# A two-layer attention and expert kernel: router weights laid over partitions by DMA, and the gate's weighting moved to another engine

## The reference

```python
logits = jnp.dot(x, Wr) + br
aff = jax.nn.sigmoid(logits)
top_v, top_i = jax.lax.top_k(aff, K)
top_w = top_v / (jnp.sum(top_v, axis=-1, keepdims=True) + 1e-09)
w_full = jnp.zeros((T, e_total)).at[jnp.arange(T)[:, None], top_i].set(top_w)
shared = jnp.dot(silu(jnp.dot(x, Wg_s) + bg_s) * (jnp.dot(x, Wu_s) + bu_s), Wd_s) + bd_s
gate = silu(jnp.einsum('th,ehi->eti', x, Wg) + bg[:, None, :])
up = jnp.einsum('th,ehi->eti', x, Wu) + bu[:, None, :]
down = jnp.einsum('eti,eih->eth', gate * up, Wd) + bd[:, None, :]
routed = jnp.einsum('te,eth->th', w_full, down)
return (shared + routed).reshape(b, s, h)
```

## Time and profile before

| What | Value |
|---|---|
| median of 3 runs | 244.21 us (244.19 to 244.49) |
| the profiled execution, its own time | 244.43 us |
| span of that execution | 242.6 us |
| PE busy | 224.3 us (92%) |
| DVE busy | 175.9 us (72%) |
| ACT busy | 128.8 us (53%) |
| POOL busy | 74.6 us (31%) |
| granted clock of TensorE, mean over the span | 0.993 |

### The profile page before, as it was taken

One profiled execution on the slowest core, in us unless ns is written; L12 is line 12 of the kernel. 1 busy time (PEld: TensorE's weight loads), 2 busy tenths in 40 slices (PEclk: granted clock), 3 DMA queues, 4 the chain that ended last, 5 costly groups with the idle time before them and its releaser, 6 DMA issues.

```text
span 242.6 us, 3703 instructions
## 1 busy us (share of the span) xinstructions
PE 224.3 (92%) x1220; PEld 157.4 (65%) x1228; DVE 175.9 (72%) x436; ACT 128.8 (53%) x262; POOL 74.6 (31%) x113
## 2 busy tenths in 40 slices
PE   8979998999997888999999998889999999999993
PEld 2446544655564344678687966667888888888871
DVE  2689766663376887796351787999888879888883
ACT  2427557678536921442544766666454555554551
POOL 6235997020430600000490303000453353353000
PEclk9999999999999999999999999979999999999999
DMA  6316739300000000000052000000112212200002
GB/s 226 123 43 195 263 87 352 118 0 0 3 0 0 1 0 4 0 0 3 1 139 80 0 3 1 0 0 0 46 43 49 81 47 48 83 0 0 3 0 86
DMA packets 6152, 12.92 MB, mean 53 GB/s; under 512 B 1139, under 2 KB 2259, under 8 KB 5878
## 3 DMA queue, kind: packets, MB, share of 16 engines
q1 hardware_dynamic: 5302, 11.91, 15.8%
q10 hardware_dynamic: 832, 0.78, 1.0%
HBM read 10.78 MB, written 0.52 MB: 47 GB/s over the span
## 4 chain that ended last, share of the span: by engine, by line
PE 74%; DVE 18%; ACT 3%; issue 3%; POOL 1%; DVEq 0%; another core or an unknown queue 0%; ACTq 0%; POOLq 0%
PE bank L1939 6%; PE bank L1943 6%; PE bank L1940 6%; PE bank L1302 5%; PE bank L1442 5%; PE bank L1428 5%; DVE att L707 4%; PE bank L1383 4%; PE bank L1973 3%; PE bank L1789 3%; PE bank L1976 3%; PE bank L1328 3%; PE bank L1974 3%; PE bank L1954 3%; PE bank L1776 3%
## 5 line engine op out<-in xcount | busy, mean ns | idle before, releaser
L1242 ACT ACTIVATE arena_d<-bank,bias 128x512 f32<-128x512 f32 x34 | 23.4, 689 | 32.3 <-PE bank L1943 32.3
L893 DVE SCALAR_TENSOR_TENSOR arena_d<-bank,bias,arena_d 128x512 f32<-128x512 f32 x34 | 25.5, 750 | 9.5 <-ACT arena_d L1242 9.2
L572 DVE TENSOR_REDUCE smax<-bank 128x3 f32<-128x462 f32 (+2 forms) x44 | 25.2, 619 | 8.4 <-PE bank L1383 8.3
L1054 ACT ACTIVATE arena_c<-bank 128x512 f32<-128x512 f32 x40 | 22.6, 598 | 10.2 <-PE bank L1442 5.4
L471 POOL CAST arena_b<-rec 128x512 fp32r<-128x512 f32 x17 | 13.4, 788 | 46.7 <-PE bank L1976 46.6
L1939 PE MATMUL bank<-arena_b 128*128 128x512 f32 x68 | 27.1, 399 | 0.1
L1943 PE MATMUL bank<-arena_b 128*128 128x512 f32 x68 | 27.1, 398 | 0.0
L1940 PE MATMUL bank<-arena_b 128*128 128x512 f32 x68 | 27.0, 397 | 0.0
L907 DVE TENSOR_TENSOR arena_a<-arena_d,arena_a 128x512 fp32r<-128x512 f32 x34 | 23.5, 691 | 0.8 <-ACT arena_a L1249 0.7
L1249 ACT CAST arena_a<-arena_d 128x512 fp32r<-128x512 f32 x34 | 20.8, 612 | 3.2 <-DVE arena_d L902 2.9
L902 DVE TENSOR_TENSOR arena_d<-arena_d,bank 128x512 f32<-128x512 f32 x32 | 21.8, 681 | 0.4 <-PE bank L1954 0.3
(11 more groups left out here) (256 smaller groups left out, 477.1 us busy)
## 6 DMA issues: line engine op xcount, KB each, us to landing
rec<-in_rec SPq DMA_DIRECT2D x17, 257.0 KB, 2.6
arena_d<-in_fc SPq DMA_DIRECT2D x1, 2048.0 KB, 9.2
fc<-in_fc SPq DMA_DIRECT2D x1, 2048.0 KB, 7.8
arena_a<-yhi SPq DMA_DIRECT2D x14, 64.0 KB, 2.0
x<-in_x SPq DMA_DIRECT2D x2, 256.0 KB, 4.2
out<-x SPq DMA_DIRECT2D x2, 256.0 KB, 2.0
arena_a<-ylo SPq DMA_DIRECT2D x7, 64.0 KB, 2.0
pack<-in_pack ACTq DMA_DIRECT2D x1, 382.0 KB, 5.6
```

Of the source, the lines that this page charges most:

```text
L572: dve.tensor_reduce(dst, src, AX.X, ALU.max).then_inc(Z["max_done"], 1)
L893: dve.scalar_tensor_tensor(to[:, k % 2, :], bank[:, 2 + k % 2, :], bias[:, u % SPLITS, 1:2], sil[:, k % 2, :], ALU.add, ALU.mult).then_inc ...
L1054: act.activation(pT[:, n % RING, :], bank[:, 3 + n % 2, :], ACT.Exp, scale=float(DH) ** -0.5)\
L1242: act.activation(sil[:, k % 2, :], bank[:, k % 2, :], f, bias=bias[:, STEPS[k][0] % SPLITS, 0:1])\
```

## The change

In the steps k = 8 to 33 ("steps 9 to 34") the matmul `router_weights` is left out. In its place:

- ACT copies the transposed router weights out of PSUM as they are (`raw_weights(b)`, in the place of `high_weights_again(b)`, whose copy goes to POOL). SP stores them into a DRAM scratch of shape (2, 32, 8, 512), eight copies of each expert's row. For each step, SP then loads a tile `laid_w` of 128x512: two experts, 64 partitions each, eight partitions from each copy. There is a ring of six such tiles and three semaphores.
- POOL multiplies `sil` by that tile, in place (`silw_ready`), and DVE's `gated(k)` takes the product in place of `sil`. `gated(k)` writes into PSUM bank 5 - k % 2, which `hidden(k)` names, and `weighted(k)` falls away. `high_hidden` and `low_hidden` read that bank.
- The splits of records 6 to 16 leave POOL: ACT casts (`high_cast`) and DVE makes the rest (`low_part`), both within the loop. `SPLITS` goes from 5 to 6, and POOL splits records 0 to 5.
- The rings of `hhi` and `hlo` go from 2 to 4, and `down` runs three steps behind `gate_and_up`, not two. `gate_and_up(k)` from k = 10 on waits for `sil_ready` for its gate and for `hh_ready` only ahead of its up part.
- The biases no longer come with the records but with the constants (`pack`, 34 more columns). Some tiles change their places, two semaphores are merged into others (`mask` into `rows`, `screst_ready` into `sclo_ready`).

```diff
@@ SP, after the constants and the first records
+            def laid_weights(k):
+                u, b = STEPS[k]
+                m = k - LAID_FROM
+                if m >= LAID_RING:
+                    sp.wait_ge(Z["hh_ready"], k - LAID_RING + 1)
+                if m >= 3:
+                    sp.wait_ge(Z["laid%d" % (m % 3)], laid_weights_count(m - 3))
+                own = wraw_d[b, 2 * (u - 1):2 * u, :, None, :].rearrange("e r j s -> (e r) j s")\
+                    .broadcast_to([2 * COPIES, I1 // COPIES, S])
+                sp.dma_start(laid_w[:, m % LAID_RING, :], own).then_inc(Z["laid%d" % (m % 3)], 16)
+            for n in range(3, SPLITS + 3):
+                record(n)
+            for b in range(B):
+                sp.wait_ge(Z["wraw_ready"], b + 1)
+                sp.dma_start(wraw_d[b], wraw[:, None, b * S:(b + 1) * S].broadcast_to([E1, COPIES, S])).then_inc(Z["stored"], 16)
+            sp.wait_ge(Z["stored"], 16 * B)
+            for k in range(LAID_FROM, NSTEP):
+                if k % 2 == 0 and SPLITS + 3 <= k // 2 + 3 < PAIRS:
+                    record(k // 2 + 3)
+                laid_weights(k)
@@ POOL, after the splits of records 0 to 5 and the four rsqrt
-            for n in range(SPLITS, PAIRS):
-                split(n)
+            for b in range(B):
+                pool.wait_ge(Z["whi_ready"], b + 1)
+                pool.tensor_copy(w3[2 * E1:3 * E1, b * S:(b + 1) * S], f32(w3[0:E1, b * S:(b + 1) * S])).then_inc(Z["w3_ready"], 1)
+            for k in range(LAID_FROM, NSTEP):
+                m = k - LAID_FROM
+                pool.wait_ge(Z["laid%d" % (m % 3)], laid_weights_count(m))
+                pool.wait_ge(Z["sil_ready"], k + 1)
+                own = laid_w[:, m % LAID_RING, :]
+                pool.tensor_tensor(own, sil[:, k % 2, :], own, ALU.mult).then_inc(Z["silw_ready"], 1)
@@ DVE, gated(k)
+                if k >= LAID_FROM:
+                    m = k - LAID_FROM
+                    dve.wait_ge(Z["silw_ready"], m + 1)
+                    dve.wait_ge(Z["hlo_ready"], k - 1)
...
+                    dve.scalar_tensor_tensor(bank[:, 5 - k % 2, :], bank[:, 2 + k % 2, :], bias[:, u, 1:2],
+                                             laid_w[:, m % LAID_RING, :], ALU.add, ALU.mult).then_inc(Z["hh_ready"], 1)
@@ DVE, new
+            def low_part(n):
+                dve.wait_ge(Z["cast_ready"], n + 1)
+                dve.tensor_tensor(wlo[:, n % SPLITS, :], rec[:, n % 3, 0:3 * P], f32(whi[:, n % SPLITS, 0:3 * P]), ALU.subtract)\
+                    .then_inc(Z["split_ready"], 1)
@@ DVE, the loop
             for k in range(8, NSTEP):
                 gated(k)
                 low_hidden(k - 1)
-                weighted(k)
+                if k % 2 == 0 and k // 2 + 2 < PAIRS:
+                    low_part(k // 2 + 2)
@@ ACT, new
+            def raw_weights(b):
+                act.wait_ge(Z["w3_ready"], 2 * (b + 1))
+                act.copy(wraw[:, b * S:(b + 1) * S], bank[0:E1, (4, 7)[b], :]).then_inc(Z["wraw_ready"], 1)
+            def high_cast(n):
+                act.wait_ge(Z["rec_ready%d" % (n % 3)], 16 * (n // 3 + 1))
+                act.wait_ge(Z["down_done"], STEPS.index((n - SPLITS, 1)) + 1)
+                act.copy(whi[:, n % SPLITS, :], rec[:, n % 3, :]).then_inc(Z["cast_ready"], 1)
@@ ACT, the loop
             for k in range(8, NSTEP):
                 silu(k)
                 high_hidden(k - 1)
+                if k % 2 == 0 and k // 2 + 2 < PAIRS:
+                    high_cast(k // 2 + 2)
@@ PE, gate_and_up(k)
                 if b == 0:
                     pe.wait_ge(Z["split_ready"], u + 1)
-                if k >= 2:
+                laid = k >= LAID_FROM + 2
+                if laid:
+                    pe.wait_ge(Z["sil_ready"], k - 1)
+                elif k >= 2:
                     pe.wait_ge(Z["hh_ready"], k - 1)
...
                 for j in range(2):
+                    if laid and j:
+                        pe.wait_ge(Z["hh_ready"], k - 1)
@@ PE, the loop
             for k in range(8, NSTEP):
                 gate_and_up(k)
-                router_weights(k)
-                down(k - 2)
+                if k > LAID_FROM:
+                    down(k - 3)
+            down(NSTEP - 3)
             down(NSTEP - 2)
```

More of the change, by code:

```diff
@@ L38 @@
 PAIRS = E1 // 2 + 1
-SPLITS = 5
+SPLITS = 6
+LAID_FROM = 8
+LAID_RING = 6
+COPIES = 8
+PARTS_RING = 4
 SIGMOIDS = 2
@@ L250, in build @@
         rec = sb("rec", [P, 3, REC])
-        bias = sb("bias", [P, SPLITS, 2])
         def f32(ap):
             return ap.bitcast(F32)
-        L = {n: sem("ld_" + n) for n in ("x0", "x1", "ctx2", "watt", "pack", "late", "rows", "gate", "fc1", "fc2", "mask", "few")}
+        L = {n: sem("ld_" + n) for n in ("x0", "x1", "ctx2", "watt", "pack", "late", "rows", "gate", "fc1", "fc2", "few")}
         names = """var_ready rstd_ready consts_ready xn_ready xnT_psum xnT_ready q_psum qhi_ready qlo_ready allhi_ready alllo_ready laid0 laid1 k_psum
@@ L311, in build, with hidden @@
         EXP_ORDER = (2, 3, 0, 1)
+        def hidden(k):
+            return bank[:, 5 - k % 2, :] if k >= LAID_FROM else hh[:, k % 2, :]
         @block.sync
@@ L320, in _ @@
             sp.dma_start(gate[:, :], gate_d).then_inc(L["gate"], 16)
-            sp.dma_start(mask[:, :, :], mask_d).then_inc(L["mask"], 16)
+            sp.dma_start(mask[:, :, :], mask_d).then_inc(L["rows"], 16)
             sp.dma_start(wout[:, :, :], wout_d).then_inc(L["few"], 16)
@@ L349, in _, with record @@
                 sp.dma_start(rec[:, n, :], rec_d[n]).then_inc(Z["rec_ready%d" % n], 16)
-            for n in range(3, PAIRS):
+            def record(n):
                 sp.wait_ge(Z["split_ready"], n - 2)
                 sp.dma_start(rec[:, n % 3, :], rec_d[n]).then_inc(Z["rec_ready%d" % (n % 3)], 16)
+            def laid_weights(k):
[18 more added lines that the diff above has]
+                laid_weights(k)
             for b in range(B):
@@ L412, in _ @@
                 expand(cc)
-            pool.wait_ge(L["mask"], 16)
+            pool.wait_ge(L["rows"], 64)
             pool.tensor_scalar(maskneg[:, :, :], mask[:, :, :], MASKED, 0.0, ALU.mult, ALU.add).then_inc(Z["maskneg_ready"], 1)
@@ L418, in _ @@
                                ALU.add).then_inc(Z["xbo_ready"], 1)
-            pool.wait_ge(L["rows"], 48)
+            pool.wait_ge(L["rows"], 64)
             pool.tensor_copy(rows3[:, :], rows[:, :]).then_inc(Z["rows_split"], 1)
@@ L1241, in silu @@
                 f = ACT.Silu if k >= SIGMOIDS else ACT.Sigmoid
-                act.activation(sil[:, k % 2, :], bank[:, k % 2, :], f, bias=bias[:, STEPS[k][0] % SPLITS, 0:1])\
+                act.activation(sil[:, k % 2, :], bank[:, k % 2, :], f, bias=bias[:, STEPS[k][0], 0:1])\
                     .then_inc(Z["sil_ready"], 1)
@@ L1246, in high_hidden @@
                 act.wait_ge(Z["hh_ready"], k + 1)
-                if k >= 2:
-                    act.wait_ge(Z["down_done"], k - 1)
-                act.copy(hhi[:, k % 2, :], hh[:, k % 2, :]).then_inc(Z["hhi_ready"], 1)
+                if k >= PARTS_RING:
+                    act.wait_ge(Z["down_done"], k - PARTS_RING + 1)
+                act.copy(hhi[:, k % PARTS_RING, :], hidden(k)).then_inc(Z["hhi_ready"], 1)
             def result(b):
@@ L1275, in _ @@
             affinities(1)
-            high_weights_again(0)
+            raw_weights(0)
             silu(2)
@@ L1282, in _ @@
             silu(4)
-            high_weights_again(1)
+            raw_weights(1)
             high_hidden(3)
@@ L2129 @@
     out = nc.dram_tensor("out_0", (P, T, D), F32, kind="ExternalOutput").ap()
-    build(nc, *args, out)
+    scratch = nc.dram_tensor("scratch", (B, E1, COPIES, S), F32).ap()
+    build(nc, *args, scratch, out)
     r = run(nc, [arrays], core_ids=[0])
```

83 lines of the change are left out of this document (44 added, 39 removed).

## The result

The kernel after the change takes 256.37 us, the median of four runs (256.29 to 257.09), against 244.35 for the kernel before on the same chip (244.19 to 244.51). The ratio is **1.0511** [1.0495, 1.0526], so 12.0 us slower, where 9.0 had been forecast; put on the 244.21 from which the forecast was counted, the ratio gives 256.7, just above the top of the range. The profiled execution took 257.09 us with a span of 255.3. PE's share of the chain, 74% before, is now 59%; DVE went from 18 to 24%, POOL from 1 to 5% and ACT from 3 to 6%.

What follows compares the result with a forecast made beforehand. PE's ten matmuls per step bound the last stage; waits for `low_part` replace them. Step 33 starts 8.45 us later, the tail makes it +8.95: 244.43 to 253.4, less 0.22 to the median, 253.2 us; range 246.8 to 256.4.

Steps and rivals of the forecast that it cites:

- What bounds the loop, and which wait replaces it: PE's ten matmuls per step bound the old loop; then PE waits at even steps 10 to 30 for DVE's `low_part`.
- As meant: Rival for the loop: weights ready whenever PE needs them, steps of 2.06 us without gaps, 238.2 us; chance 0.07.
- No block: Rival for the loop: `low_part` is not held up by POOL's product, pairs of 4.88 us, 247.2 us; chance 0.13.
- More is late: Rival: PE's clock falls in the loop (two pairs give 257.6 us) or tiles come over 1.3 us late; chance 0.12.
- A pair takes 5.48 us: Two loop steps on PE, with `low_part` held up until 0.40 after POOL's product: 5.48 us instead of 4.59.
- Its second product is early: 4.7 us: First pair, steps 8 to 10: no `down` in step 8, so POOL's second product comes early and the pair takes 4.7 us.
- ten pairs, steps 10 to 30: Loop from the start of step 10 to step 30: ten pairs of 5.48 us, 54.8 us.
- first pair: Loop from the start of step 8 to step 10: 4.7 us.
- tail, from step 33's start: End of kernel: `down(32)`'s third matmul waits for `low_hidden(32)` until 4.26 after step 33's start; +0.5 us, between 0 and 0.8.
- step 8's start, three last steps: Step 8 starts at 175.15 us; the three steps from step 30 to step 33 take 0.11 + 6.18 us.

Runs made afterwards that it cites:

- experiment 1: Changed kernel with only DVE's `low_part` moved to the head of its turn, ahead of `gated` and `low_hidden`: 238.88 us, ratio 0.979 to the kernel before.
- experiment 3: Changed kernel with `low_part` replaced by a reduction over the same 384 columns, reading one SBUF operand: 251.82 us, ratio 1.0333 to the kernel before.
- Experiment 5: Changed kernel with only `low_hidden(7)` moved ahead of `gated(8)` on DVE: 255.80 us, ratio 1.0484 to the kernel before.
- experiment 7: Changed kernel with `low_part` first, then `gated`, `low_hidden`; only `low_hidden(32)` ahead of `gated(33)`; `laid_w` 8 bytes further on: 237.56 us, ratio 0.9736 to the kernel before.
- experiment 6: Changed kernel with DVE's order `low_hidden`, `low_part`, `gated` in every turn and `laid_w` 8 bytes further on: 242.47 us, ratio 0.9941 to the kernel before.
- experiment 4: Changed kernel with the `laid_w` tiles 8 bytes further on: 254.79 us, ratio 1.0445 to the kernel before; with 64 or 32 bytes, 256.46 and 256.67 us.

## Why the prediction was right in direction and too small

**What bounds the loop, and which wait replaces it: right.** PE stands before each even step from 10 to 30 but step 12, released by `low_part`, ten waits in the list; at step 12 there are only 0.33 from matmul to matmul. `low_part` ends 0.41 after POOL's product. DVE, ACT and POOL are each below three quarters busy (at most 7.03 of 10 us from 190 to 200 us, DVE), and experiment 1 removes all of it by order alone.

**The rivals.** "As meant" fell because `low_part` stands where the forecast read it. It is what experiment 1 turns the change into: 238.88, where 238.2 had been worked out. "No block" fell by the rows of the timeline, and with experiment 3 it can be told what its world would have taken: 251.8, not 247.2. Its pairs take 5.26, not 4.88: on that path lie POOL's product (1.29 for 1.18), the handover to it (0.14 for 0.05), and the one from it to DVE (0.21 for 0.05). "More is late" was seen only at one place, a lower clock behind one wait of 2.09 us, for 0.2 us; no transfer was late.

**The sum: too small by 3.7 us** (257.09 - 244.43 = 12.66 in the profiled executions, 8.95 forecast). Two steps of the working failed. "A pair takes 5.48 us" had the path right and sizes on it too small: measured 5.73, two thirds of the 3.7. "Its second product is early: 4.7 us" left out a wait: measured 5.73, most of the rest. The terms that were mis-sized:

| term | forecast | measured | makes |
|---|---|---|---|
| ten pairs, steps 10 to 30 | 54.8 | 57.27 | +2.47 |
| first pair | 4.7 | 5.73 | +1.03 |
| tail, from step 33's start | +0.5 | +0.86 | +0.36 |
| step 8's start, three last steps (6.26 for 6.29), outside the span | | | -0.15 |

*The pairs.* Small terms, 0.25 together in the pair shown, add up ten times. POOL's product was taken as 1.18 and is 1.27 there, 1.29 in the mean: it has the length of the upper end, 0.966 scaled by columns, and not that of the straight line between two other widths. The handover from ACT to POOL was taken as 0.05 and is 0.14 (silu at 201.29 for 0.69, POOL at 202.12). The restart of PE, 2.21 instead of 2.17, is the third; three other links are 0.01 longer each.

*The first pair.* Here a wait was missing, not only a size. The 4.7 gave `low_hidden` no turn with POOL, as is right where it reads a PSUM bank; that of step 7 reads SBUF, and POOL holds it up just as it later holds up `low_part`. From the product's end to step 10 it takes 1.07 so (179.73 to 180.80), not the 0.40 + 0.05 of the forecast, which is 0.62 of what is missing; the rest is the late silu (0.27) and the longer handover and product (0.09 each); together 1.07, since the forecast's terms add up to 4.66, put as 4.7. Experiment 5 moves this instruction and wins 0.51. In experiment 3, where `low_part` has no turn to wait for, the first pair still takes 5.73 (174.53 to 180.26). Rows for it were at hand: L907 stretched by POOL to 0.82 and 0.84.

*The tail.* The wait was the right one. PE's timeline, the start of step 33 and the matmul that waits:

```profile
244.33 0.39 PE L2005 MATMUL bank<-arena_b 128*128 128x512 f32 x1
...
249.00 0.50 PE L2044 MATMUL bank<-arena_a,arena_b 128*128 128x512 f32 x1 [1.07 <-DVE arena_a L953]
```

The third matmul of `down(32)` stands 1.07 us for `low_hidden(32)` behind `gated(33)`, and comes 4.67 us after step 33's start, where 4.26 and a handover had been worked out. POOL's product, the 0.14, and 0.21 from POOL to DVE's `gated` instead of 0.05 make up the 0.36. The last matmul of `down(33)` is 5.91 after that start (5.03 before). With `low_hidden(32)` put first, and the 8 bytes, it is 5.22 (experiment 7).

The medians differ by 12.0, less than the 12.66, because the profiled execution of the change is 0.7 longer than its other runs: its step 8 starts 0.48 later than in experiment 5 (175.07 and 174.59), whose instructions are the same up to there: the granted clock from 155 to 160 us is 0.69 in the one and 1.00 in the other. The stretch at the lower clock behind step 10 gives 0.2 more.

## What to carry to other kernels

When work is moved to another engine, read each in-order queue as a list and ask what now stands ahead of the instruction that the bounding engine waits for: here 17.5 us lay between two orders of the same instructions (256.37 and 238.88). Put what somebody is waiting for ahead of what itself waits, but check which wait the old order was covering, as experiment 6 shows. In a chain that is passed through ten times, a handover or a tenth of a microsecond of an unmeasured instruction is a term like any other; give each its own bound.

## What the runs showed of the hardware

The length of POOL's two-input operation depends on where its operands lie: 1.29 us for 128x512 with the tiles as they were, 1.09 with one of them 8 bytes further on, 1.29 again at 32 and 64 bytes. The kernel before agrees at 384 columns: its ring of records goes on by 2056 bytes, so the second place stands 8 bytes and the third 16 bytes further on modulo 32, and the splits from the second place take 0.86 to 0.87 us, those from the first and the third 1.00 to 1.02. Which engine or memory rule makes it was not tried.

On this path a handover to or from POOL took longer than the one from DVE to PE: 0.14 us from ACT to POOL and 0.20 from POOL to DVE, against 0.06 from `low_part` to PE. And a wait of 1.3 us on PE in every pair of steps, 7.38 of 10 us busy, left the granted clock at 1.00, while behind the one wait of 2.09 us it was at the lower level for some 3 us in this execution. The wait alone does not bring that about: in experiment 4's run with 64 bytes PE stands 2.09 us at the same step (until 180.37), its next matmuls are 0.34 and 0.24 apart and the granted clock from 180 to 184 us is 1.00; in the run with 32 bytes, behind a wait of 2.08 us, it is 0.50 from 182 to 184. What decides between the two was not found.
